# Statistics of the projection's norm made inside odd tiles of the second attention

## The reference, cut to what matters

```
x = x + _L1_xattn_ref(_layernorm(x), ctx_1024, Wq, Wk, Wv, Wp, bp, ln_g, ln_b)   # the second attention
x = x + _L1_ffn_ref(_layernorm(x), in_proj_w, in_proj_b, ...)                    # begins with a projection

def _layernorm(x, axis=-1, eps=1e-05):
    m = jnp.mean(x, axis=axis, keepdims=True)
    v = jnp.var(x, axis=axis, keepdims=True)
    return (x - m) / jnp.sqrt(v + eps)

# first lines of _L1_ffn_ref
qkv = src @ in_proj_w.T + in_proj_b
q, k, v = jnp.split(qkv, 3, axis=-1)
```

## Time and profile before

| what | value |
|---|---|
| median of 3 runs | 1347.45 us (1343.01 to 1347.97) |
| profiled execution | 1353.44 us |
| its span | 1351.7 us |
| PE busy | 1124.3 us (83%) |
| PEld busy | 945.0 us (70%) |
| DVE busy | 765.7 us (57%) |
| ACT busy | 418.7 us (31%) |
| POOL busy | 497.9 us (37%) |
| last instruction of the second attention (DVE L411) | starts at 495.43 us, 0.42 us long |
| first product of the projection (PE L1486) | starts at 508.73 us |

### The profile page before, as it was taken

One profiled execution on the slowest core, in us unless ns is written; L12 is line 12 of the kernel. 1 busy time (PEld: TensorE's weight loads), 2 busy tenths in 40 slices (PEclk: granted clock), 3 DMA queues, 4 the chain that ended last, 5 costly groups with the idle time before them and its releaser, 6 DMA issues.

```text
span 1351.7 us, 20740 instructions
## 1 busy us (share of the span) xinstructions
PE 1124.3 (83%) x7405; PEld 945.0 (70%) x7405; DVE 765.7 (57%) x1719; ACT 418.7 (31%) x869; POOL 497.9 (37%) x453
## 2 busy tenths in 40 slices
PE   6889698886588869899974999999993699876896
PEld 4778576674367755598864999999973577763564
DVE  3667767665467654788871222222239587638583
ACT  2445432222255631111111222222231244440365
POOL 4434511336446502276856111001325344310242
PEclk9789899999689989799986999999996699987798
DMA  7999000000100020000034432211212000000001
GB/s 281 386 387 386 3 0 1 21 1 0 75 1 1 1 88 1 1 1 9 32 115 176 161 115 80 98 39 49 83 47 59 1 1 1 1 1 1 0 24 40
DMA packets 43733, 93.59 MB, mean 69 GB/s; under 512 B 3822, under 2 KB 17807, under 8 KB 40839
## 3 DMA queue, kind: packets, MB, share of 16 engines
q1 hardware_dynamic: 35254, 62.24, 12.8%
q0 software_dynamic: 7104, 29.14, 6.0%
q10 hardware_dynamic: 1296, 1.18, 0.3%
HBM read 39.02 MB, written 51.51 MB: 67 GB/s over the span
## 4 chain that ended last, share of the span: by engine, by line
PE 69%; DVE 16%; issue 5%; ACT 5%; POOL 4%; DMA 1%; POOLq 0%; SPq 0%; DVEq 0%; ACTq 0%
PE PS L1949 10%; PE PS L1959 9%; PE PS L870 8%; PE PS L1832 4%; PE PS L1217 4%; PE PS L853 3%; PE PS L883 3%; PE PS L1486 3%; PE PS L843 3%; PE PS L825 2%; PE PS L1821 2%; PE PS L738 2%; PE PS L822 1%; PE PS L1858 1%; PE PS L1207 1%
## 5 line engine op out<-in xcount | busy, mean ns | idle before, releaser
L1949 PEld LDWEIGHTS PS<-scr 128*128 128x128 f32 x992 | 119.4, 196 | 5.2 <-issue 1.8
L1949 PE MATMUL PS<-scr 128*128 128x128 f32 x992 | 121.4, 280 | 1.5 <-issue 1.4
L588 POOL TENSOR_TENSOR scr<-scr,big 128x1232 f32<-128x1232 f32 x32 | 72.0, 2249 | 131.1 <-DVE big L396 131.1
L1982 ACT ACTIVATE scr<-PS,W 128x128 f32<-128x128 f32 x148 | 53.5, 367 | 193.6 <-PE PS L1949 193.6
L1959 PE MATMUL PS<-scr 128*128 128x256 f32 x496 | 112.2, 379 | 0.0
L691 ACT ACTIVATE big<-PS 128x512 f32<-128x512 f32 x144 | 74.5, 525 | 94.2 <-PE PS L853 94.0
L853 PE MATMUL PS<-W,scr 128*128 128x128 f32 x480 | 83.2, 297 | 21.4 <-ACT scr L686 8.1
L2012 DVE TENSOR_SCALAR scr<-PS,W 128x128 f32<-128x128 f32 x148 | 51.4, 350 | 86.5 <-PE PS L1949 86.4
L1959 PEld LDWEIGHTS PS<-scr 128*128 128x128 f32 x496 | 91.8, 190 | 11.2
L870 PEld LDWEIGHTS PS<-scr,big 128*128 128x128 f32 x640 | 85.3, 200 | 7.4 <-issue 5.7
L870 PE MATMUL PS<-scr,big 128*128 128x34 f32 (+1 forms) x640 | 87.5, 279 | 0.0
(11 more groups left out here) (407 smaller groups left out, 2430.1 us busy)
## 6 DMA issues: line engine op xcount, KB each, us to landing
expert_in<-zeros SPq DMA_DIRECT2D x1, 19712.0 KB, 55.2
expert_out<-zeros SPq DMA_DIRECT2D x1, 19712.0 KB, 106.6
scr<-ew_in POOLq DMA_DIRECT2D x12, 1024.0 KB, 6.6
scr<-expert_in SPq DMA_DIRECT2D x38, 128.0 KB, 2.1
big<-ew_in POOLq DMA_DIRECT2D x4, 1024.0 KB, 8.9
expert_out<-scr POOLq DMA_DIRECT2D x28, 128.0 KB, 2.0
W<-pack SPq DMA_DIRECT2D x1, 2458.0 KB, 8.8
W<-pack SPq DMA_DIRECT2D x1, 2152.0 KB, 8.4
```

What stands on the lines that cost most here:

```text
L588: g.tensor_tensor(sc3, sc3, a_mx[u % 3].unsqueeze(2).broadcast_to([P, H, S2]), ALU.subtract).then_inc(s["sub_ready"], 1)
L1949: ins = pe.matmul(bank(1 + f % 4, G), e_w1[slot][:, k, f * P:(f + 1) * P], e_xT[:, k, :], start=(k == 0), stop=(k == C - 1))
L1982: a.activation(e_h[:, f, :], bank(1 + f % 4, G), ACT.Relu, bias=moe_bias(e, f)).then_inc(s["h_act"], 1)
```

## The change

The 16 tiles' statistics are no longer made in one piece at the start of the projection. A function `qkv_stats(v, ch, k)` makes them for one sample (two `bn_stats`, a wait for them, two `bn_aggr`), and `qkv_rstd(g, k)` makes the rstd of one sample on POOL with `power` (an addition and a power on two values a partition). In the second attention DVE calls the first for sample `i - 1` in the odd tiles from the fourth on (`i` = 1 to 7, so samples 0 to 6), between `normed` or `head_normed` and `scores`; POOL calls the second in the same tiles. Sample 7 is done in the projection, behind the normed sample 0. The buffers lie in `small` and not in `scr`, and PE's release of `zT_psum` stands ahead of its first wait.

```diff
@@ att_dve
+            def attended_stats(k):
+                v.wait_ge(s["y_done"], PTILE(1, 2 * k + 1) + 1)
+                qkv_stats(v, ch, k)
...
                 if lay == 1 and not odd and i + 2 < B:
                     query_vars(i + 2)
+                if lay == 1 and odd and i >= 1:
+                    attended_stats(i - 1)
                 if u + 2 < NT:
                     scores(u + 2)
@@ att_pool
                 if not odd and i + AHEAD[lay] + 1 < B:
                     rstd_of(i + AHEAD[lay] + 1)
+                if lay == 1 and odd and i >= 1:
+                    qkv_rstd(g, i - 1)
@@ buffers
-        q_stats = cut(NT * 6).rearrange("p (n s) -> p n s", n=NT)
-        q_mv = cut(NT * 2).rearrange("p (n s) -> p n s", n=NT)
-        q_rstd = cut(NT)
+        q_stats = [csmall(T * 6).rearrange("p (t s) -> p t s", t=T) for _ in range(2)]
+        q_mv = csmall(NT * 2).rearrange("p (n s) -> p n s", n=NT)
+        q_ve = csmall(NT)
+        q_rstd = csmall(NT)
@@ projection
+        def qkv_stats(v, ch, k):
+
+            for t in range(T):
+                ch.inc(v.bn_stats(q_stats[k % 2][:, t, :], X[:, T * k + t, :]))
+            ch.sync()
+            for t in range(T):
+                ins = v.bn_aggr(q_mv[:, T * k + t, :], q_stats[k % 2][:, t, :])
+            ins.then_inc(qkv["var_ready"], 1)
+
+        def qkv_rstd(g, k):
+            g.wait_ge(qkv["var_ready"], k + 1)
+            power(g, q_rstd[:, T * k:T * k + T], q_ve[:, T * k:T * k + T], q_mv[:, T * k:T * k + T, 1]).then_inc(qkv["rstd_ready"], 1)
+
         def qkv_dve(v, ch):
...
-            for n in range(NT):
-                ch.inc(v.bn_stats(q_stats[:, n, :], X[:, n, :]))
-            ch.sync()
-            for n in range(NT):
-                ch.inc(v.bn_aggr(q_mv[:, n, :], q_stats[:, n, :]))
-            ch.sync()
-            v.tensor_scalar(q_rstd, q_mv[:, :, 1], EPS, None, ALU.add).then_inc(s["var_ready"], 1)
-            v.wait_ge(s["rstd_ready"], 1)
-            v.wait_ge(s["bias_ready"], 1)
-
             def norm(j, r):
...
+            v.wait_ge(s["rstd_ready"], B - 1)
             norm(0, 0)
+            qkv_stats(v, ch, B - 1)
+            v.wait_ge(s["rstd_ready"], B)
+            v.wait_ge(s["bias_ready"], 1)
             qkv_samples(v, body)
 
         def qkv_pool(g):
             s = qkv
             g.sem_inc(s["z_kept"], 2)
-            g.wait_ge(s["var_ready"], 1)
-            g.tensor_tensor(q_rstd, q_rstd, neghalf[:, 0:NT], ALU.pow).then_inc(s["rstd_ready"], 1)
+            qkv_rstd(g, B - 1)
...
         def qkv_pe(pe):
             s = qkv
             in_w = kc("in_w", 3 * D)
+            pe.sem_inc(s["zT_psum"], 2)
             pe.wait_ge(in_w2, 16)
...
-            pe.sem_inc(s["zT_psum"], 2)
```

## The result

The changed kernel takes 1343.99 us (median of 20 runs) beside 1350.26 us for the kernel before (20 runs): a ratio of 0.9956, 95% interval 0.9935 to 0.9976, or 3 to 9 us less. Timed again on another occasion it was 0.9936 (0.9909 to 0.9964), 1342.54 beside 1348.76 us. Forecast were 8.5 us, a ratio of 0.9937.

The account below looks back on a forecast made before the run. Nearly 11 us at the seam between second attention and projection, where PE has only bias rows, were taken as the bound. 8.5 from the seam, 0 from tiles, 0 from the clock: 1347.45 - 8.5 = 1338.9 us, range 1333 to 1344.5.

Parts of the forecast that it names:

- Seam: Between second attention and projection: first product at 500.20 in place of 508.73, 8.5 us less, ACT's bias copies waited for last.
- The clock's term: First products of the projection: same lower-clock loss before and after, 0; bounds a gain of 1.25 us, a loss of 0.8 to 1.
- first rival: At the projection's first products the full clock comes back earlier: 9.8 us less, 1337.7 us; chance 0.10.
- Sum: Whole kernel: 8.5 us from the seam, 0 from tiles, 0 from the clock; 1338.9 us, 0.63% less.
- likeliest case: Whole kernel: the forecast of 8.5 us less, chance 0.70, with the range 1336 to 1341.5 us.
- Tiles, DVE: Odd tiles of the second attention: 0.94 us of added DVE work each, hidden by cover, cost 0; bound 4.7 us.
- second rival: In the odd tiles DVE's delay does reach PE: only 3.8 us less, 1343.6 us; chance 0.07.
- Tiles, POOL: Odd tiles: one `power` of 1.78 us in each of seven, 3.1 us of slack left, cost 0; bound 7.1 us.
- fourth rival: In the attention POOL's `power` pushes `query_rstd` past its slack: 2.4 us more than before, 1349.8 us; chance 0.03.
- Sample 1: Projection's start: sample 1 normed by 501.3 after POOL's `power`, wanted by PE at 504.2; cover 2.9 us, cost 0.
- third rival: The seam gives less, through weight loading or sample 1's cover: 3 to 4 us lost, 1342.5 us; chance 0.10.

Follow-up runs that it names:

- filled kernel: Kernel before, with 40 products that nobody reads put into PE's wait between the bias products and the first transposes; ratio 0.9967 (0.9936 to 0.9999).
- Three makings: Changed kernel with the statistics of samples 0 to 6 made three times over in the odd tiles; one run, 1344.37 us.
- six makings: Changed kernel with the statistics of samples 0 to 6 made six times over in the odd tiles; one run, 1381.41 us.
- release kernel: Changed kernel with PE's release of `zT_psum` put back behind its four bias products; one run, 1345.67 us.

## Why the prediction was right or wrong

It was right that the kernel gets faster, by the seam and nothing else. The clock, a term taken as nothing, was the one that was mis-sized. By its steps:

**Seam.** The last wait is the one it named, ACT's bias copies. Said were 4.35 us from the residual to the first product, measured 4.70. The four bias products took 496.78 - 494.34 = 2.44 us until the transposes started, 2.15 said: the clock had its lower level from 496 on, earlier than before. So 12.88 - 4.70 = 8.2 in place of 8.5.

**The clock's term,** taken as 0, was -0.5. The lower level lasted some 3.8 us from the first product in place of 2.5, and the first group took 4.71 us in place of 4.20. That was within the bounds given; the first rival, an earlier return, went the other way. The step said that the lower level doesn't come from PE's wait and that the change would not remove its cause. It was there again, beginning among the bias rows. What the cause is was not settled: 128-row bias products kept the level at 1.00 in the changed kernel, but it also fell after short waits and in a long one, without one-row products. The Trainium skill, "TensorE: Matmul & The Clock Gate", Part 1, says that activity releases the throttle. The filled kernel agrees, 1.00 by 498 with PE kept at work on 128 rows; the changed kernel shows that one-row products did not keep it there though they kept PE busy.

**Sum.** 8.2 and then 7.7 at the second group, for 8.5. Timed were 0.44% and 0.64%, and both intervals hold 7.7 / 1350.3 = 0.57%. A gain so near the bound of 0.5% deserved a lower chance than 0.72 of being beyond it: the first timing gave 0.44%. The time itself, 1343.99 us, lies in the range of 1333 to 1344.5 by only 0.5 us, and outside the likeliest case's 1336 to 1341.5. Of the 5.1 us between it and 1338.9, 2.8 are the start: three runs of the kernel before had the median 1347.45, twenty had 1350.26.

**Tiles, DVE.** Right: pairs of 16.09 us and 2.35 us of idle time left, where 2.0 were said. Three makings used that up and cost nothing there; six cost 3.4 us a pair, of which the lower clock is a part. So the second rival falls. But the cover was read in the middle tiles alone. The last tiles have 0.35 us of idle time ahead of the scores made in tile 13, and three makings lost 4.8 us there, more than half of it at the lower clock. The prediction had no line for them.

**Tiles, POOL.** 3.88 us are left, 3.1 said, because this L189 takes 0.19 us, and not the 0.99 of the row that stood for it. The row was an exception: the 80 of the kernel before have a median of 0.19 us, and L189 is as short right behind another instruction of POOL as after a wait, here in the changed kernel behind a power of 5.43 us:

```profile
359.10 0.19 POOL L189 TENSOR_TENSOR big<-big,small 128x2 f32<-128x2 f32 x1
```

Why three of them in the middle tiles take 0.98 to 0.99 is open. The fourth rival, the slower one, was far off: 1.1 us of 5.01 were used.

**Sample 1.** Its normed rows end at 500.2 and its transposes start at 503.39: cover 3.2, said 2.9. DVE's wait ahead of them ended on ACT's last bias copy (L1469) and not on POOL's power, as was said, for the power was done 0.8 us sooner. Of the third rival's 3 to 4 us only the 0.8 above were lost, by the clock and not by transfers or a wait.

**A reason that did no work:** the prediction has DVE free to norm sample 0 "since PE's release of `zT_psum` now stands ahead of its wait". Put back behind the bias products, it took effect 0.35 us after the first of them began.

## What to carry to other kernels

When work sits at the seam between two stages, ask which part of it the next stage's first item needs: the gain came from sample 0 no longer waiting for the other samples, and not from hiding the rest in the tiles. Read the cover for added work in the tightest tiles, the last ones, and not in the steady ones alone. Count a seam's gain up to the second group, for the clock can give back part of it in the first.

## What the runs showed of the hardware that was not expected

- PE's semaphore release, placed behind four bias products in its program, took effect 0.35 us after the first of them started, a group of 2.07 us: it was not held until the products ahead of it ended.
- POOL's addition over 128x2 (L189) took 0.19 us as a median, after a wait or right behind another instruction, but 0.98 to 0.99 in three middle tiles of the second attention, right behind the bias (L566, now L572). The cause is open.
- The clock fell to 0.50 as the one-row bias products began, during them or soon after in all profiles that have them, but for the release kernel and the six makings, where it was down before. With 128-row ones it stayed at 1.00 in three profiles of four. It fell as well in tiles without any: in the kernel with three makings about 1 us after a wait of 1.4 us, and in two kernels by 490, next to waits that left it at 1.00 in others. That a short wait of PE costs more than itself is therefore suggested by one place, 4.8 us lost for 2.1 us of delay, and not shown.
- Two profiles of one program differ by 3 us (486.2 and 489.1) from the expert stage to the gates, so a gain of a few microseconds is to be read at its place and not from spans.
